# Attention with 16 heads on one core: VectorE's share of the score exponentials in five pairs of 1024 columns a unit, taken from the common score buffers, with one weighted sum a round

## The reference

```
xn = layernorm(x)
q, k, v = xn @ w.T + b for each of the three, split into 16 heads of 16 columns; q / 4
scores = q @ k.T            # 4096 x 4096 for each head
attn = softmax(scores)      # over the keys, in float32
ctx = attn @ v              # 4096 x 16 for each head
out = x + (ctx @ out_w.T + out_b) + fp8_linear(xn, weight, bias)
```

## Time and profile before

| what | value |
|---|---|
| median of three runs | 1961.01 us |
| the profiled execution | 1961.78 us |
| its span, first to last instruction | 1960.0 us |
| mean granted TensorE clock | 0.992 |
| ScalarE busy | 1812.5 us |
| TensorE busy with matmuls | 1912.2 us |
| VectorE busy | 1274.3 us |
| before the first exponential | 134.0 us |
| after the last exponential | 49.9 us |

### The profile page before, as it was taken

How to read it: one execution, slowest core, us unless ns; L and a number is a source line. 1 busy time by engine, 2 the same in 40 slices (tenths; PEclk the granted TensorE clock), 3 DMA queues, 4 the chain that set the end, 5 groups by cost and what they waited for, 6 DMA issues and landing times.

```text
span 1960.0 us, 39423 instructions
## 1 busy us (share of the span) xinstructions
PE 1912.2 (98%) x14963; PEld 687.3 (35%) x14963; DVE 1274.3 (65%) x1789; ACT 1812.5 (92%) x1993; POOL 44.2 (2%) x53
## 2 busy tenths in 40 slices
PE   5969999999999999999999999999999999999998
PEld 3623333333333333333333333333333333333337
DVE  6645765756566765756566765756566666656567
ACT  2339999999999999999999999999999999999991
POOL 2000000000000000000000000000000000000000
PEclk9979999999999999999999999999999999999999
DMA  7880111203021121203011121203011121203014
GB/s 198 270 250 3 25 31 26 31 10 47 9 34 15 25 31 26 31 10 47 10 31 18 25 31 26 31 10 47 9 27 22 25 31 26 31 10 47 10 21 109
DMA packets 65632, 83.87 MB, mean 43 GB/s; under 512 B 9952, under 2 KB 47360, under 8 KB 62208
## 3 DMA queue, kind: packets, MB, share of 16 engines
q1 hardware_dynamic: 65472, 81.58, 20.4%
HBM read 54.79 MB, written 26.21 MB: 41 GB/s over the span
## 4 chain that ended last, share of the span: by engine, by line
PE 93%; SPq 2%; DMA 1%; DVE 1%; ACT 1%; issue 1%; ACTq 0%
PE banks L1121 48%; PE banks L1100 36%; PE banks L1128 3%; PE banks L1011 2%; PE banks L1232 1%; PE banks L1022 1%; DVE o_sb L824 1%; ACT probs L608 1%; DMA k_parts<-probs 1%; PE banks L1058 1%; PE banks L1078 0%; DMA q_st<-q_parts 0%; PE banks L1216 0%; SPq L305 0%; PE banks L1224 0%
## 5 line engine op out<-in xcount | busy, mean ns | idle before, releaser
L608 ACT ACTIVATE probs<-banks 128x1024 f32<-128x1024 f32 x1920 | 1769.6, 1162 | 11.0 <-PE banks L1100 5.7
L1121 PE MATMUL banks<-probs,v_st 128*32 128x512 f32 x7680 | 1026.9, 607 | 5.6 <-DVE o_sb L824 5.4
L1100 PE MATMUL banks<-q_st,k_st 50*128 50x512 f32 x4096 | 814.4, 457 | 5.3 <-ACT probs L608 4.3
L1100 PEld LDWEIGHTS banks<-q_st,k_st 50*128 50x128 f32 x4096 | 361.2, 184 | 698.3 <-ACT probs L608 629.1
L856 DVE SCALAR_TENSOR_TENSOR horner<-horner,bits 128x1024 f32<-128x1024 f32 x256 | 313.6, 1225 | 8.8
L843 DVE TENSOR_SCALAR bits<-banks 128x512 int32<-128x512 f32 x256 | 176.9, 691 | 135.0 <-PE banks L1100 119.1
L1121 PEld LDWEIGHTS banks<-probs,v_st 128*32 128x32 f32 x7680 | 151.3, 108 | 321.1 <-issue 203.4
L824 DVE STREAM_TRANSPOSE o_sb<-banks 128x512 f32<-128x512 f32 x32 | 22.9, 717 | 311.6 <-PE banks L1121 311.6
L861 DVE SCALAR_TENSOR_TENSOR d_probs<-horner,powers 128x1024 f32<-128x1024 f32 x128 | 156.8, 1225 | 97.8 <-PE banks L1128 94.5
L852 DVE SCALAR_TENSOR_TENSOR horner<-bits 128x1024 f32<-128x1024 f32 x128 | 156.9, 1226 | 4.4
L1128 PEld LDWEIGHTS banks<-d_probs,v_st 128*32 128x32 f32 x2048 | 66.6, 110 | 153.2 <-issue 153.2
(11 more groups left out here) (90 smaller groups left out, 450.1 us busy)
## 6 DMA issues: line engine op xcount, KB each, us to landing
k_st<-k_parts SPq DMA_DIRECT2D x204, 128.0 KB, 4.4
q_st<-q_parts SPq DMA_DIRECT2D x204, 64.0 KB, 4.6
q_parts<-probs SPq DMA_DIRECT2D x9, 512.0 KB, 6.3
k_parts<-probs SPq DMA_DIRECT2D x9, 512.0 KB, 6.5
xnT_copy<-probs SPq DMA_DIRECT2D x8, 512.0 KB, 4.4
probs<-xnT_copy SPq DMA_DIRECT2D x8, 512.0 KB, 6.7
w_f<-xnT_copy SPq DMA_DIRECT2D x16, 256.0 KB, 5.3
out_dram<-horner SPq DMA_DIRECT2D x16, 256.0 KB, 2.1
```

The lines of the kernel that those rows point to most:

```text
L608: act.activation(probs[:, at:at + WIDE * CHUNK].rearrange("p (t c) -> p t c", t=WIDE), banks[:, bank:bank + WIDE, :], ACT.Exp, scale=1.0 / ...
L1100: return pe.matmul(out, k_mm[rows, kt * P:(kt + 1) * P], blocks[rows, qb // GROUPS], start=True, stop=True)
L1121: last = pe.matmul(banks[VCOLS * qb:VCOLS * (qb + 1), 6, :], v_st[:, kt, :], probs[:, at:at + CHUNK], start=first_one, stop=last_one, tile ...
```

## The change

Parts of the diff; what it leaves out is named after it. `h`, `u` are head and unit, `HP` is 128, the pairs of a head.

Constants and orders. A unit has 64 pairs (`PAIRS`), all of which go through the three score buffers; `D_AT` says which places of the order are VectorE's and `D_PAIRS` which pairs (key row, half) stand there.

```diff
     GT = UG // P
     LOADS = 16 * GROUPS * TERMS
-    ROW_LOADS = 16 * GROUPS * PARTS
-    D_ROWS = (KT // 2 - 1, KT - 1)
-    A_ROWS = [kt for kt in range(KT) if kt not in D_ROWS]
-    D_SLOTS = ((2, 4, 6, 14), (16, 24, 34, 36))
-    D_PIECES = 4
-    D_SUM = ((27, 29, 31, 33), (49, 51, 53, 55))
+    BLOCKS = P // (PARTS * UT)
+    ROW_LOADS = 16 * GROUPS * PARTS * BLOCKS
+    PAIRS = KT * QB // WIDE
+    D_AT = (8, 20, 32, 44, 56)
+    D_PAIRS = ((KT // 2 - 1, 0), (KT // 2 - 1, 1), (KT - 1, 0), (KT - 1, 1), (KT - 2, 0))
+    D_STEPS = 5
+    D_BLOCKS = len(D_PAIRS)
     HALF = 2 * CHUNK
-    MAX_SLOTS, MAX_TURN = (38, 40), 46
-    UT4 = QB * len(A_ROWS)
-    UE = UT4 // WIDE
-    HT, HE = UNITS * UT4, UNITS * UE
+    MAX_ROUNDS = (6, 7)
+    AE = PAIRS - D_BLOCKS
+    HP, HE, HD = UNITS * PAIRS, UNITS * AE, UNITS * D_BLOCKS
+    SLOTS = RING // WIDE
     AK = CHUNK // UT
     SCALE = float(DH) ** -0.5
     UNIT = LOG2E * 2.0 ** 23
...
+        ORDER = []
+        for kt in range(KT):
+            for j in range(QB // WIDE):
+                if (kt, j) not in D_PAIRS:
+                    if len(ORDER) in D_AT:
+                        ORDER.append(D_PAIRS[D_AT.index(len(ORDER))])
+                    ORDER.append((kt, j))
+        PLACE = {pair: p for p, pair in enumerate(ORDER)}
+        A_PLACES = [p for p in range(PAIRS) if p not in D_AT]
+        A_INDEX = {p: a for a, p in enumerate(A_PLACES)}
+        FROM_HALF_1 = min(p for p, (kt, j) in enumerate(ORDER) if kt >= KT // 2)
+        HALF_0_READ = max(p for p, (kt, j) in enumerate(ORDER) if kt < KT // 2)
+        FIRST_READ = max(p for p, (kt, j) in enumerate(ORDER) if kt == 0)
+
+        SUM_ROWS = []
+        for s_at in range(KT):
+            left = [kt for kt in range(KT) if kt not in SUM_ROWS]
+            SUM_ROWS.append(min(left, key=lambda kt: max(PLACE[kt, j] + (12 if (kt, j) in D_PAIRS else 0)
+                                                         for j in range(QB // WIDE))))
+        SUM_AT = {kt: s_at for s_at, kt in enumerate(SUM_ROWS)}
```

```diff
+                def buffer_free(h, n):
+
+                    if c.full and n < BUFS:
+                        pe.wait_ge(c.exp_done, h * HE + EXP_0)
+                        pe.wait_ge(c.d_taken, h * HD + D_0)
+                        return
+                    if not c.full and h * HP + n < BUFS:
+                        return
+                    back, m = divmod(n - BUFS, HP)
+                    u, p = divmod(m, PAIRS)
+                    if p in D_AT:
+                        pe.wait_ge(c.d_taken, h * HD + (D_0 + back * HD + u * D_BLOCKS + D_AT.index(p) + 1))
+                    else:
+                        pe.wait_ge(c.exp_done, h * HE + (EXP_0 + back * HE + u * AE + A_INDEX[p] + 1))
...
+                def sampled_maxima(h, u, g):
+
+                    v, nxt = 1 - u, h + u
+                    if g == 0:
+                        pe.wait_ge(c.q_in[v], nxt * LOADS + LOADS)
+                        pe.wait_ge(c.k_first, nxt * LOADS + LOADS)
+                    max_part(v, g, h * UNITS + u, h * UNITS + (u + 2))
+
+                def sampled_heads():
+
+                    for r in range(HEADS * HP // 2):
+                        nxt = [divmod(n, HP) for n in (2 * r + LEAD, 2 * r + LEAD + 1) if n < HEADS * HP]
+                        for h, n in nxt:
+                            arrivals(h, n)
+                        for i, (h, n) in enumerate(nxt):
+                            scores(h, n)
+                            u, at = r // (PAIRS // 2), r % (PAIRS // 2)
+                            if i == 0 and at in MAX_ROUNDS:
+                                sampled_maxima(u // UNITS, u % UNITS, MAX_ROUNDS.index(at))
+                        if r:
+                            unit, at = divmod(r - 1, KT)
+                            weighted_sum(unit // UNITS, unit % UNITS, at)
+                    weighted_sum(HEADS - 1, UNITS - 1, KT - 1)
+
```

```diff
-                    dve.wait_ge(c.misc_free, job + 2)
+                    if n:
+                        dve.wait_ge(c.d_chain, steps)
+                    dve.wait_ge(c.st_done, h * HP + (pair + 1))
+                    dve.tensor_scalar(words.rearrange("p (t c) -> p t c", t=WIDE), banks[:, bank:bank + WIDE, :],
+                                      -EXP_BIAS, EXP_BIAS, ALU.max, ALU.add).then_inc(c.d_taken, 1)
+                    dve.wait_ge(c.d_taken, done + (D_0 + 1))
+                    if n:
+                        dve.wait_ge(c.d_ready, done)
...
+                def unit_sampled(h, u):
+                    unit = h * UNITS + u
+                    links = c.links_before(h, u)
+                    d_block(h, u, 0)
+                    maxima(unit + 1, 1 - u, links)
+                    links += MAX_LINKS
+                    d_block(h, u, 1)
+                    if unit:
+                        check_sums(unit - 1, links)
+                        links += 1
+                    if u:
+                        scale_inputs(h)
+                    d_block(h, u, 2)
+                    if u:
+                        round_inputs(h)
+                    d_block(h, u, 3)
+                    if u:
+                        store_inputs(h)
+                    d_block(h, u, 4)
+                    sums(h, u, links)
+
```

The negative maxima are transposed by VectorE in blocks of 32x32 and not by TensorE, and loaded by 16 transfers a unit and not 4; the first 128 keys are a load of their own (`k_first`), six transfers:

```diff
+            def load_k(c, head, piece):
+                rows = bass.ds(head * DH, DH)
+                cols = (slice(P, S // 2), slice(S // 2, S), slice(0, P))[piece]
                 for i_term, i in enumerate(K_TERMS):
                     for g in range(GROUPS):
                         at = g * GROUP + i_term * DH
-                        sp.dma_start(k_st[at:at + DH, cols], k_dram[i, rows, cols]).then_inc(c.k_in[half], 16)
+                        sp.dma_start(k_st[at:at + DH, cols], k_dram[i, rows, cols]
+                                     ).then_inc((*c.k_in, c.k_first)[piece], 16)
 
             def load_rows(c, u, count):
                 sp.wait_ge(c.row_ready, count)
                 for i in range(PARTS):
                     for g in range(GROUPS):
-                        at = g * GROUP + KROWS + i
-                        sp.dma_start(q_st[at:at + 1, u * UG:(u + 1) * UG].rearrange("o (t c) -> o t c", c=P),
-                                     neg_row[i * UT + g * GT:i * UT + (g + 1) * GT, :]).then_inc(c.row_in[u], 16)
+                        at, r0 = g * GROUP + KROWS + i, i * UT + g * GT
+                        to = q_st[at:at + 1, u * UG:(u + 1) * UG].rearrange("o (t b x) -> o b t x", t=GT, x=PARTS * UT)
+                        for b in range(BLOCKS):
+                            first_row = b * PARTS * UT + r0
+                            sp.dma_start(to[:, b], neg_row[first_row:first_row + GT, :]).then_inc(c.row_in[u], 16)
 
```

More of the change, by code:

```diff
@@ L252, in program @@
         ACC_0 = 1
+        D_0 = 1
         OUT_0 = 16
@@ L293, in program, with sums_before_reuse, span @@
+        SUMMED = [1 + max(SUM_AT[kt] for kt in range(half * (KT // 2), (half + 1) * (KT // 2))) for half in range(2)]
+        def sums_before_reuse(a):
+            before, a = divmod(a - SLOTS, HE)
+            u, a = divmod(a, AE)
+            return before * STEPS + u * KT + SUM_AT[ORDER[A_PLACES[a]][0]] + 1
+        def span(start, count):
+            return slice(start, start + count) if isinstance(start, int) else bass.ds(start, count)
         tok = "(t p) d -> p t d"
@@ L937, in outputs @@
+                if c.full:
+                    with dve.Fori(0, HEADS) as h:
+                        head_full(h)
+                    dve.wait_ge(c.chain, c.links_before(HEADS, 0))
+                else:
+                    for h in range(HEADS):
+                        for u in range(UNITS):
+                            unit_sampled(h, u)
+                    check_sums(HEADS * UNITS - 1, c.links_before(HEADS, 0))
             def outputs(again):
@@ new lines, in scores @@
+                def scores(h, n):
+                    u, p = divmod(n, PAIRS)
+                    kt, j = ORDER[p]
+                    bank = WIDE * ((n if c.full else h * HP + n) % BUFS)
+                    blocks = q_mm[:, u * UG:(u + 1) * UG].rearrange("k (c j x) -> k j c x", j=QB // GROUPS, x=P)
+                    buffer_free(h, n)
+                    for g in range(GROUPS):
+                        rows = slice(g * GROUP, g * GROUP + STACK)
+                        last = pe.matmul(banks[:, bank + g, :], k_mm[rows, kt * P:(kt + 1) * P], blocks[rows, j],
+                                         start=True, stop=True)
+                    last.then_inc(c.st_done, 1)
@@ L1149, in attend @@
                                 pe.wait_ge(c.q_in[0], LOADS)
-                                pe.wait_ge(c.k_in[0], LOADS)
+                                pe.wait_ge(c.k_first, LOADS)
                                 pe.wait_ge(v_done, V_0 + 2 * NCH)
-                            max_part(0, g, 0, 1, ready=False)
-                JOB0 = c.max_jobs + 1
-                for e in range(LEAD):
```

(9 more changed lines are left out.)

432 lines of the change are left out of this document (183 added, 249 removed).

## The result

| | before | after |
|---|---|---|
| median, us | 1960.82 | 1985.33 |
| runs, us | 1957.46 to 1964.19 | 1984.69 to 1986.28 |
| span of the profiled execution, us | 1960.0 | 1982.9 |

The ratio is 1.0125, with a 95% interval from 1.0107 to 1.0143: slower by 1.25%, as forecast (1984). The span grew by 22.9 us; the sum had +23.1.

A forecast was written before the change was run, and what follows sets the result against it. ScalarE was taken to bound the kernel, almost without a gap. Per unit 54.08 + 1.43 + 0.35 = 55.86 us, +17.6 over 32 units, plus 5.5 before the loop, gave 1984 us; range 1950 to 2010.

The forecast's parts named there:

- One exponential less: ScalarE, each unit: 59 exponentials of 0.9166 us instead of 60, 54.08 us, 1.22 under the 55.30 of now.
- Five gaps of 0.29: ScalarE stands still 0.29 us at each of five VectorE blocks, 1.43 us a unit; bounds 0.20 and 0.40 each.
- a second wait in the middle of a sum: TensorE's weighted sum, a row having two sources: no row prices it; it could raise each gap up to 0.40 us.
- Maxima 0.35: Rounds 6 and 7: the maxima's parts make TensorE late at the block at 20, 0.35 us more gap; bounds 0 to 0.45.
- The 0.31 that a unit of before lost: ScalarE before the change: 60 exponentials take 54.99 us of a unit's 55.30, so 0.31 us is lost.
- The unit: Whole loop unit: 54.08 + 1.43 + 0.35 = 55.86 us, 0.55 more than 55.30; 32 units +17.6 us.
- VectorE: VectorE's blocks of 7.8 us fit: first instruction about 1.23 us, never held more than 1.4 us.
- Before the loop: Prologue: sixteen row transfers and k's added loads delay the first exponential, +5.5 us together, bounds +2 to +10.
- k's six added loads: Prologue, SyncE's queue: 2.8 us of issues, mostly behind landings, counted as 0.8 us.
- No gap: Rival: ScalarE sheds its exponential and no gap opens; unit 54.4 us, total 1938; chance 0.13.
- gain and gap cancelled: Rival: gaps at the lower bound cancel the gain; unit 55.1 us, total 1960; chance 0.09.
- TensorE bound: Rival: the second wait inside each sum makes TensorE bind; unit 56.9 us, +51, total 2017; chance 0.14.

The follow-up runs named there:

- e1: Changed kernel with four VectorE pairs a unit instead of five, the one at place 56 dropped, ScalarE taking 60 exponentials: 2005.4 us.
- e2: Changed kernel with the weighted sum cut to 8 of 512 columns in five rounds a unit, those making VectorE's scores; no candidate: 1975.49 us.
- e3: Changed kernel with sums cut to 8 of 512 columns in those five rounds and each following one, ten a unit; no candidate: 1945.18 us.
- e4: Changed kernel with the next unit's maxima in rounds 6 and 10 instead of 6 and 7, VectorE's maxima and sums check swapped: 1978.25 us.
- e5: Changed kernel with ten of a unit's 32 row sums, around the VectorE pairs, issued in two halves by columns: 2043.17 us.

## Why the prediction was right

- *What binds.* ScalarE, in both kernels. Every kernel here whose unit changed did so by ScalarE's count and gaps, until the halved sums made TensorE the longer one.
- *One exponential less.* 59 at 0.9165, as in 59 at 0.9166 of the forecast; with both short sums the unit is bare 54.08.
- *Five gaps of 0.29.* Measured 0.30, one behind each pair (161 stops). e1 shows that the gap belongs to the pair, e2 and e3 that it is the chain over the sum and not VectorE's hold. (The prediction has 0.29 by one way and 0.92 - 0.64 = 0.28 by the other; that is rounding.) The upper bound for a second wait in the middle of a sum wasn't needed.
- *Maxima 0.35.* Measured 0.345, at place 21 alone; e4 takes two thirds of it away by putting rounds between the parts.
- *The 0.31 that a unit of before lost.* The sum dropped it without a reason. By the same reckoning on before's trace it stands at the exponentials 43 and 45 of a unit (intervals of 0.995 and 1.05, just behind the maxima's halves) and, by 0.01 to 0.05 each, at 55, 57 and 59. In after what the maxima cost is the 0.345, and the rest is gone; no run says what held it.
- *The unit.* 55.91 against 55.86. Over 31 units that is 31 x 0.61 = 18.9 us more than before. They take 55.90 to 55.93 each, so the loads inside the loop were hidden, as said.
- *VectorE.* First instruction 1225 ns for 1.23; no hold.
- *Before the loop.* First exponential 8.2 us later, where I had 5.5 (bounds 2 to 10). The rows' issues were right (11.1 us for 16, against 10.9), and the rows' part was 5.5 for 4.7. Mis-sized was the term for k's six added loads: 0.8, on the ground that they stand mostly behind landings. They cost 3.4: everything behind them moved, the row transfers from 120.45 to 123.80. The Trainium skill, "DMA: Bandwidth & Descriptors", section "Bandwidth", says that transfers under 64 KB are dominated by their descriptors. The trace agrees as far as it goes: a row transfer of 1 KB takes SyncE 0.69 us in after, and one of 4 KB took 0.73 in before (2.93 for four).
- *The first unit,* for which the sum had no term of its own, was shorter: 57.95 us, before 61.58 (to the end of its last exponential, from 0.92 us before the end of its first). The 3.6 us go with TensorE's clock at the loop's start, below. They aren't the change's: e5, with the changed prologue, has a long first unit too.
- *Behind the loop* 49.3 us and not 49.9.
- *The total was right in part by luck.* Measured, 18.9 + 8.2 - 3.6 - 0.6 = 22.9; the forecast had 17.6 + 5.5 = 23.1, the first of them over all 32 units. The unit's part is 1.3 us over the forecast and the prologue's 2.7; the first unit and the end, which nobody had forecast, took back about as much. The mechanism of the unit doesn't rest on that.
- *The rivals.* No gap, and gain and gap cancelled: ruled out by the 0.30 at each place. TensorE bound: not here (it waits for ScalarE ahead of pairs all along), but near enough to spoil a cure.
- Gap, place and size follow from the chain over three buffers. The Trainium skill, "Perfetto Trace Analysis", section "Optimization Strategy", says that the same gap repeating on the engine that should be saturated can mean too few buffers. The trace fits that (the gap stands behind each of the 160 pairs), but that a fourth buffer would cure it no run shows, since none was tried. Nor was a bank of its own for VectorE's tiles, with two accumulators kept.

## What to carry to other kernels

Work taken off the bounding engine is worth its time only less what its place in the shared buffers takes away: count, at each point, how much of the bounding engine's work lies between a buffer's release and its next use. Here, with three buffers, each item that another engine took shortened that cover from three items to two, and shortening one link of the chain only brought the next one out; for other numbers of buffers it is not shown. And a sum can be right by two errors of opposite sign, so compare it term by term.

## What the hardware showed that I had not expected

- *TensorE's clock at the loop's start.* It stood at the lower level (0.50, 1.2 GHz) when the loop began, after a stretch with little work (in after it was busy 2.6 us of the 10 before 145), and how long it stayed there differed between executions of kernels with the same prologue. After, and below it the kernel with halved sums, both with the first exponential at about 142:

```profile
145.00:150.00 5.00, 4.77 (x20) 0.50 0.07 14
150.00:155.00 5.00, 5.00 (x34) 0.87 0.10 39
155.00:160.00 5.00, 5.00 (x52) 1.00 0.00 0
```

```profile
145.00:150.00 5.00, 4.88 (x24) 0.50 0.14 36
150.00:155.00 5.00, 5.00 (x34) 0.50 0.04 17
155.00:160.00 5.00, 5.00 (x30) 0.56 0.00 0
```

  The first unit exceeds the later ones by 1.1 to 2.6 us in twelve of the traces and by 5.8 and 6.3 in two (halved sums, and the kernel before). It goes with the time that the clock stayed low: in the twelve the upper level came 7.5 to 13.6 us behind the start of the first exponential, in the two 17.5 and 17.3 (in before from 134.0 to 151.3). What decides between them I can't say; it isn't the start of the loop alone, since 142.2 had 2.0 and 141.9 had 5.8. The times of the kernel before move with the clock too: of its 38 executions beside these runs, the 17 with a mean granted clock of 0.995 or more took 1954.0 to 1959.6 us, and the 16 with 0.991 or 0.992 took 1959.1 to 1965.0. Its profiled execution (0.992) is like the latter.
- *A change between score and sum matmuls costs TensorE time.* 0.33 us for one more change there and back in a round, with the same columns in all and eight more weight loads (1.99 against 1.66). What part the weight loads have isn't shown.
- *GpSimd issues small transfers faster than SyncE did.* The 16 row transfers took it 8.52 to 8.55 us in six traces (0.53 each), and SyncE 11.09 in after (0.69 each).
